# Bias products of a feed-forward layer as pairs in two 32-row tiles of TensorE, issued at the end of each pair of tiles

## The reference

```python
x = layernorm(x + attention(x))          # q, k, v, o with low-rank updates and biases
x = layernorm(x + q_times_decayed_scan)  # element-wise recurrence over ctx * ctx
x = layernorm(x + ffn(x))

def ffn(x):                              # inner = 2048
    h = silu(bitlinear158(x, w1, b1))
    h = layer_norm(gelu(h), ln_g, ln_b)
    return bitlinear158(h, w2, b2)

def bitlinear158(x, w, b):
    xq = act_quant(rms_norm(x))          # rounded to -128..127, one scale for each position
    wq = weight_quant(w)                 # -1, 0, 1 times one scale
    return einsum('bsd,od->bso', xq, wq) + b
```

## Time and profile before

| | |
|---|---|
| median of three executions | 1051.52 us |
| the profiled execution, its own time | 1050.39 us |
| its span (first to last instruction) | 1048.6 us |
| TensorE busy | 950.2 us, 91% |
| VectorE busy | 891.9 us, 85% |
| ScalarE busy | 827.4 us, 79% |
| GpSimd busy | 605.4 us, 58% |
| from the start of one f stage to the next, in the middle of the run | 58.0 to 58.3 us |

### The profile page before, as it was taken

The page is one execution under the profiler, slowest core; times in us unless marked ns, Lnnn a source line. Parts: engine busy times, 40 slices in busy tenths (PEclk is TensorE's granted clock), DMA queues, the critical chain, the costliest instruction groups (busy, mean ns, idle before and its releaser), DMA issues.

```text
span 1048.6 us, 23525 instructions
## 1 busy us (share of the span) xinstructions
PE 950.2 (91%) x9388; PEld 655.1 (62%) x9388; DVE 891.9 (85%) x1474; ACT 827.4 (79%) x957; POOL 605.4 (58%) x767
## 2 busy tenths in 40 slices
PE   5998997999999999999999999999999999978416
PEld 3766756676767767676767767676767677644102
DVE  4577868989898999989898989899898989995766
ACT  3646686888979797988888797978889797977684
POOL 2332337474766749485757658494757566572653
PEclk9999998999999999999999999999999999988668
DMA  9432200213122121323131121323231321122213
GB/s 357 158 111 113 72 3 21 74 52 84 23 71 61 43 76 52 84 52 83 35 100 23 56 68 44 83 52 84 52 84 21 79 56 54 42 52 63 53 30 91
DMA packets 106352, 73.68 MB, mean 70 GB/s; under 512 B 91386, under 2 KB 91386, under 8 KB 104451
## 3 DMA queue, kind: packets, MB, share of 16 engines
q1 hardware_dynamic: 105522, 70.34, 24.2%
q10 hardware_dynamic: 720, 1.84, 0.5%
HBM read 41.73 MB, written 8.40 MB: 48 GB/s over the span
## 4 chain that ended last, share of the span: by engine, by line
PE 60%; DVE 26%; DMA 6%; ACT 4%; issue 3%; POOL 1%; SPq 0%; POOLq 0%; DVEq 0%; ACTq 0%
PE bank L1333 21%; PE bank L1467 11%; PE bank L1474 9%; DMA xqT<-xq 5%; PE wave L1382 4%; PE bank L1396 4%; PE wave L1358 3%; DVE neg_max L962 3%; DVE h L1085 3%; PE bank L1400 3%; DVE stats L1013 3%; PE bank L1468 3%; DVE fz L1090 2%; DVE rows L1029 2%; DVE qx L1052 1%
## 5 line engine op out<-in xcount | busy, mean ns | idle before, releaser
L962 DVE TENSOR_REDUCE neg_max<-wave 128x8 f32<-128x2048 f32 x64 | 146.2, 2284 | 39.0 <-PE wave L1358 39.0
L547 POOL TENSOR_TENSOR h<-h,g_tile 128x2048 f32<-128x2048 f32 x30 | 139.9, 4663 | 39.1 <-ACT h L738 39.1
L655 ACT ACTIVATE probs<-wave 128x1024 f32<-128x1024 f32 x128 | 124.4, 1024 | 40.5 <-PE wave L1382 40.3
L1467 PE MATMUL bank<-w,xqT 128*128 128x512 fp8e4 x496 | 129.7, 384 | 20.6 <-DMA xqT<-xq 20.6
L437 POOL TENSOR_SCALAR attn_hi<-attn 128x256 fp32r<-128x256 f32 x64 | 31.8, 497 | 150.1 <-DVE attn L995 134.8
L717 ACT ACTIVATE h<-bank,qx 128x512 f32<-128x512 f32 x124 | 83.8, 689 | 24.4 <-PE bank L1468 22.1
L693 ACT ACTIVATE rows<-rows,rstd 128x512 f32<-128x512 f32 x96 | 74.3, 807 | 33.1 <-POOL rstd L453 18.5
L1085 DVE TENSOR_TENSOR h<-h,b_tile 128x2048 f32<-128x2048 f32 x32 | 84.0, 2624 | 17.0 <-POOL h L547 16.9
L1467 PEld LDWEIGHTS bank<-w,xqT 128*128 128x128 bf16 x496 | 47.8, 99 | 78.0 <-issue 17.4
L1474 PE MATMUL bank<-w,hqT 128*128 128x512 fp8e4 x416 | 94.3, 380 | 0.0
L496 POOL TENSOR_TENSOR rows<-rows,bo_tile 128x512 f32<-128x512 f32 x32 | 52.6, 1665 | 71.2 <-DMA rows<-x 71.2
(11 more groups left out here) (181 smaller groups left out, 2844.1 us busy)
## 6 DMA issues: line engine op xcount, KB each, us to landing
ctx_sb<-ctxT SPq DMA_DIRECT2D x16, 512.0 KB, 3.8
rows<-x SPq DMA_DIRECT2D x16, 512.0 KB, 4.0
out<-rows SPq DMA_DIRECT2D x32, 256.0 KB, 2.5
xT_in<-xT SPq DMA_DIRECT2D x15, 512.0 KB, 4.7
h<-w1T SPq DMA_DIRECT2D x4, 1024.0 KB, 14.6
h<-w2T SPq DMA_DIRECT2D x4, 1024.0 KB, 4.8
h<-Wq SPq DMA_DIRECT2D x1, 1024.0 KB, 6.2
h<-Wk SPq DMA_DIRECT2D x1, 1024.0 KB, 9.8
```

What stands on the lines that cost most here:

```text
L547: po.tensor_tensor(h_of(b, q)[:, :], h_of(b, q)[:, :], g_tile[:, :], ALU.mult).then_inc(done, 1)
L655: ac.activation(probs[:, kt, :, :], wave[:, :, kt * T:(kt + 1) * T], ACT.Exp, scale=SM_SCALE).then_inc(S["probs_ready"], 1)
L962: dv.tensor_reduce(neg_max[:, :, :], wave[:, :, :].rearrange("p j (t k) -> p j t k", t=NT), axis=AX_X, op=ALU.max, negate=True).then_inc(S ...
L1467: pe.matmul(p[:, :], xqT[:, q, kc, :], w1[:, kc, n * FW:(n + 1) * FW], start=(kc == 0), stop=False)
```

## The change

The bias rows are kept twice, on partitions 0 to 31 and on 32 to 63: the scale's parts stand in columns 512 to 520 and 544 to 552 of `xq`, and the bias's parts in rows 0 to 8 and 32 to 40 of `b1_rows`. An even tile issues its four matmuls and nothing else. The odd tile behind it issues its four, and then two bias matmuls of 32 rows, the first on rows 0 to 31 into the even tile's bank, the second on rows 32 to 63 into its own. Each ends its accumulation and raises `f_ready`.

```diff
-                for k in range(NPART):
-                    sp.dma_start(b1_rows[k * NPART:(k + 1) * NPART, :], b1_scratch).then_inc(u_b1_in, 16)
+                for g in range(2):
+                    for k in range(NPART):
+                        at = g * HD + k * NPART
+                        sp.dma_start(b1_rows[at:at + NPART, :], b1_scratch).then_inc(u_b1_in, 16)
...
                 for k in range(NPART):
-                    part = xq[:, :, D + NPART * k:D + NPART * (k + 1)]
-                    done(dv.tensor_copy(part, left.unsqueeze(2).to_broadcast([P, NT, NPART])))
+                    part = xq[:, :, D:D + 2 * HD].rearrange("p q (g r) -> p q g r", g=2)
+                    part = part[:, :, :, NPART * k:NPART * (k + 1)]
+                    done(dv.tensor_copy(part, left.unsqueeze(2).unsqueeze(3).to_broadcast([P, NT, 2, NPART])))
...
-                f_product(take(j, "f", u, "xqT_loaded", j - 1, 16), u)
-
-            def f_product(p, u):
+                take(j, "f", u, "xqT_loaded", j - 1, 16)
+                f_product(j - 1, u)
+
+            def f_product(b, u):
                 q, n = divmod(u, NF)
+                p = bank_of("f", u, b)
                 for kc in range(KC):
                     pe.matmul(p[:, :], xqT[:, q, kc, :], w1[:, kc, n * FW:(n + 1) * FW], start=(kc == 0), stop=False)
-                pe.matmul(p[:, :], xqT[:, q, KC, :], b1_rows[:, n * FW:(n + 1) * FW], start=False,
-                          stop=True).then_inc(S["f_ready"], 1)
+                if u % 2:
+                    for g in range(2):
+                        at = slice(g * HD, (g + 1) * HD)
+                        pe.matmul(bank_of("f", u - 1 + g, b)[:, :], xqT[at, q, KC, :],
+                                  b1_rows[at, (n - 1 + g) * FW:(n + g) * FW], start=False,
+                                  stop=True).then_inc(S["f_ready"], 1)
...
-                    pe.wait_ge(u_b1_in, 16 * NPART)
+                    pe.wait_ge(u_b1_in, 16 * 2 * NPART)
```

More of the change, by code:

```diff
@@ L1485, in drain_f @@
                 wait(pe, reader, b, count_read)
-                f_product(bank_of("f", u, LAST), u)
+                f_product(LAST, u)
             def drain_y(b, q):
```

## The result

| | before | changed |
|---|---|---|
| time, median of four runs each | 1051.73 us | 1060.54 us |
| range of the runs | 1050.95 to 1052.96 | 1059.59 to 1062.35 |
| profiled execution, its span | 1050.39, 1048.6 | 1060.69, 1058.9 |
| mean round, f stage of body 3 to that of body 14 | 58.10 | 58.44 |

What follows compares the result with a forecast made beforehand. TensorE's ring bounds the kernel, a ScalarE ring 0.13 us behind. 13 rounds x (0.39 + 0.04) = 5.6, plus 1.04 at body 2 and drain starts, plus 0.45 in the drain, = 7.1: 1058.6 us, range 1056 to 1061.5.

Steps and rivals of the forecast that it cites:

- The price of changing mode: TensorE's f stage: changes between full array and row tiles cost 0.86 us up to the last pair, all the stage gained.
- dear pair: Rival: each pair's weight load on TensorE is exposed, 0.10 instead of 0.015, giving 1064.3 us; chance 0.16.
- half price: Rival: only one direction of the mode change costs, some 0.4 a round, giving 1052.4 us; chance 0.12.
- faster side: Rival: the change of mode on TensorE costs nothing, giving 1047.9 us; chance 0.16.
- TensorE's gain: TensorE gains only what `shifted` no longer pays for the mode change, about 0.2 us a round.
- The results: Both results of a pair come at its end, so the last silu on ScalarE starts 0.52 us later.
- The second ring: Last silu, gelu, h_var, g_mul, z_add, L1130: just behind TensorE's ring, it takes over, carrying the 0.52 us delay.
- The slack in front of L1130: VectorE's L1130 waits 0.13 us for TensorE, so a 0.52 delay at z_add leaves 0.39 at L1130.
- Behind L1130: Second layernorm, quantise_x, the DMA and f simply follow L1130's 0.39 us delay each round.
- The first two rounds: f stages of bodies 1 and 2 cost what all do: 0.52 at body 2's start, and 0.43 a round.
- The last stretches: The drain's start, where TensorE waits for the last silu, takes the full 0.52 us, as does body 2's start.
- The casts: Three casts on the ring's path write 12 elements instead of 6, costing 0.04 us a round.

Runs made afterwards that it cites:

- experiment 3: The kernel before with each bias matmul alone in one 32-row tile, in the old order: 1078.88 us, ratio 1.0233.
- experiment 8: The changed kernel with the second gelu over 1024 of its 2048 columns, the other half left out: 1050.48 us, ratio 0.9991.
- experiment 6: The kernel before with a spare 512-column activation on ScalarE between the last silu and the first gelu: 1059.03 us, ratio 1.0068.
- experiment 4: The changed kernel with ScalarE's wait for u_tern in bodies 1 and 2 moved behind the f_ready wait, freeing the table load: 1059.72 us, ratio 1.0056.
- experiment 1: The kernel before with only the change's bias-row DMAs and wider casts, the f stage as before: 1055.16 us, ratio 1.0008.
- experiment 9: The kernel before with only the last bias matmul of a loop's f stage in a 32-row tile: 1053.69 us, ratio 1.0004.
- experiment 11: The kernel before with half of the second gelu left out and a spare 512-column activation put in ahead of the gelus: 1046.99 us, ratio 0.9961.

## Why the prediction was right, and where it was not

- **The price of changing mode.** Right. Four pairs cost TensorE what they save: 0.31 and 0.32 stand around a pair, and a single tile costs 0.21 (experiment 3). Neither the dear pair nor the half price came true, and the faster side, which decided from a price under 0.4 a round, met 0.75 (the 8.55 up to the last pair, less 35 slots of 0.215 and the 0.27 of the transposes). TensorE's gain was put at about 0.2; it is 0.27 by experiment 8. Its parts are not those of the prediction: `shifted` does not wait for the last pair's slot to end and starts 0.38 earlier, but it does not run "at full pace" behind it (three sets take 0.46 as before, so the 0.10 put down to its fp32 loads stayed), and y starts 0.11 later behind it.
- **The results.** Right to 0.03: behind f they come at 2.20, 4.36, 6.77 and 8.93 for 2.21, 4.35, 6.80 and 8.94 forecast. Silu 0 starts at 2.24 for 2.25, silu 7 at 9.55 for 9.57.
- **The second ring.** Right in mechanism: it carries 0.49 to `z_add`, and experiment 6 delays L1130 as much without touching TensorE. `z_add` was to be idle for 1.8 and is for 2.08, since VectorE's work ahead of it ends 0.26 earlier.
- **The slack in front of L1130.** The term was mis-sized. I took 0.13 from the pause between L979 and L1130. But 0.49 at `z_add` became 0.28 at L1130 in the rounds shown (0.26 in the mean), so it was 0.21 or more, because L1133 starts 0.79 behind the start of the first of L981's two operations and so ahead of the recorded end of the second (642.93). The recorded end isn't the earliest start of what follows. So L1130 came 0.13 a round earlier than the 0.39 forecast.
- **Behind L1130.** The prediction said that everything from there on follows. The two small operations that `attn_lo` meets took 0.09 a round more, which it did not have, and this hid most of the error above: +0.335 came of two misses, and that it is near +0.43 is in part luck.
- **The first two rounds.** This is the step that failed. The prediction let the f stages of bodies 1 and 2 cost what all do (0.52 with the wait at the start of body 2, and 0.43). They cost 2.4 and 1.7, since the table load of silu stands behind the first result there, 1.28 on the path (experiment 4 took away 1.65 and 1.26). The order of waits showed it: in these bodies the load, not the activation, carried the wait for `f_ready`.
- **The last stretches.** "Each takes the full 0.52" was 1.0 short for body 15. By the comparison of traces above, its longer time at half clock makes 1.4 of the 1.5, and the change itself some 0.15 in place of 0.52.
- **The casts.** 0.04 a round were forecast; 0.006 a cast is 0.02, and experiment 1 gives at most 0.06.

So the 8.8 us measured against 7.1 are errors that partly cancel: ordinary rounds 1.0 too dear in sum, and 4.2 too little in the three odd places of the traces (whose difference, 10.3, is itself more than that of the medians). The direction and the ring were understood; that the totals are so near is partly luck.

## What to carry to other kernels

Price a packing of small matmuls by the changes of mode around each group, not by the matmuls saved: here one group of two between full-array work came out at nothing, and only the group that stood beside others in the same mode gained. When products are gathered at the end of a group, follow the reader of the first one, and look what ring stands behind the one that is being shortened and by how much. Before crediting a round's change to the part that was edited, split the round at a fixed instruction: here small operations far behind it gave or took 0.1 to 0.4 as their start moved against another engine's. And count the first and the last loop body apart: their waits, table loads and clock are not those of the middle.

## What the runs showed of the hardware that was not expected

- A VectorE operation on 8 columns with two operands in SBUF took 4.45 us instead of 0.17, the whole length of a GpSimd operation on 2048 columns that had started 0.10 before it. Removing half a gelu brought the two together and made the kernel 7% slower.
- The same on a small scale: beside GpSimd's `attn_lo` (0.74) VectorE's two-column operations take 0.47 to 0.75 in place of 0.16 or 0.17, among them one with a single operand (L1058, 0.59). They cost 0.14 a round more in experiment 9, which had gained 0.11, and their absence gave experiment 11 its 0.39.
- A pair of 32-row bf16 matmuls over 512 columns starts within 0.01 and takes one slot; the next 32-row matmuls start 0.01 behind it (615.31 to 615.32), without waiting for that slot to end. A change of mode in and out takes 0.21 between such a matmul and full-array ones with fp8 data.
